# A decoder layer with experts on one core: the tile loop's boundary, the drain's order, and who numbers the tiles

## What is computed

```
xn = _rms_norm(x, scale)
ids = jnp.argmin(_dist2(xn, centroids), axis=-1)
out = jnp.zeros_like(x)
for e in range(N_EXPERTS):
    h = jnp.einsum('bsd,dh->bsh', xn, up_w[e])
    a, g = jnp.split(h, 2, axis=-1)
    y = jnp.einsum('bsh,hd->bsd', a * jax.nn.silu(g), down_w[e])
    out = jnp.where((ids == e)[..., None], y, out)
return out + skip
```

## Time and profile before

| | |
|---|---|
| median of 3 runs | 1331.92 us (1331.41 to 1334.74) |
| the profiled execution, its own time | 1330.11 us |
| its span, first to last instruction | 1328.4 us |
| mean granted TensorE clock | 0.958 |
| busy: TensorE / VectorE / ScalarE / GpSimd | 90% / 64% / 47% / 32% |
| phase 1 without its last two turns | 0 to about 1016 us |
| turns B + 2 and B + 3 | about 1016 to 1062 us |
| routing | about 1062 to 1087 us |
| tiles | about 1087 to 1328 us |

### The profile page before, as it was taken

How to read it: one execution, slowest core, us unless ns; L and a number is a source line. 1 busy time by engine, 2 the same in 40 slices (tenths; PEclk the granted TensorE clock), 3 DMA queues, 4 the chain that set the end, 5 groups by cost and what they waited for, 6 DMA issues and landing times.

```text
span 1328.4 us, 29974 instructions
## 1 busy us (share of the span) xinstructions
PE 1193.5 (90%) x9698; PEld 950.0 (72%) x9699; DVE 847.7 (64%) x2193; ACT 626.5 (47%) x1297; POOL 419.5 (32%) x714
## 2 busy tenths in 40 slices
PE   5496999999999999999999999999997438898887
PEld 4274878777787878778787877778786327777776
DVE  4737667777777867777787777777764752322232
ACT  3426455564746556464746556474634412222222
POOL 2310314232231423233141423223132424444543
PEclk9598999999999999999999999999999559999999
DMA  8502530303123130303213030312257001212221
GB/s 268 130 1 112 222 112 17 113 16 111 47 79 108 34 111 16 111 16 111 79 48 126 16 111 16 111 44 91 89 194 258 31 25 53 65 61 65 62 64 42
DMA packets 51769, 112.30 MB, mean 85 GB/s; under 512 B 7333, under 2 KB 38863, under 8 KB 44944
## 3 DMA queue, kind: packets, MB, share of 16 engines
q1 hardware_dynamic: 45456, 96.81, 21.6%
q0 software_dynamic: 5616, 14.43, 3.7%
q10 hardware_dynamic: 656, 0.52, 0.1%
HBM read 89.72 MB, written 22.94 MB: 85 GB/s over the span
## 4 chain that ended last, share of the span: by engine, by line
PE 76%; DVE 10%; issue 6%; ACT 5%; POOL 2%; DMA 1%; DVEq 0%; ACTq 0%; SPq 0%; POOLq 0%
PE bank L1623 69%; PE bank L1658 3%; DVE a_p L1376 2%; PE bank L1824 2%; ACT shared L867 2%; PE bank L1997 1%; ACT a_p L862 1%; PE bank L1964 1%; POOL shared L979 1%; DVE shared L1549 1%; DVE b_ql L1274 1%; DVE a_split L1301 0%; DVE a_split L1302 0%; DVE a_split L1300 0%; DVE a_ss L1311 0%
## 5 line engine op out<-in xcount | busy, mean ns | idle before, releaser
L1623 PE MATMUL bank<-shared 128*128 128x256 f32 (+4 forms) x1728 | 323.1, 379 | 23.6 <-DVE shared L1549 13.6
L1623 PEld LDWEIGHTS bank<-shared 128*128 128x128 f32 (+2 forms) x1728 | 223.0, 168 | 84.7 <-issue 44.8
L1376 DVE TENSOR_TENSOR a_p<-a_p,eb 128x385 f32<-128x385 f32 x256 | 125.9, 555 | 75.4 <-ACT a_p L862 75.4
L1043 POOL TENSOR_SCALAR a_rz<-a_ms 128x2 f32<-128x2 f32 x16 | 3.1, 192 | 407.0 <-ACT a_sq L890 407.0
L862 ACT ACTIVATE a_p<-bank 128x385 f32<-128x385 f32 x256 | 105.1, 504 | 44.7 <-PE bank L1623 44.6
L1586 DVE TENSOR_TENSOR shared<-bank,shared 128x512 f32<-128x512 f32 x39 | 27.0, 692 | 121.7 <-ACT shared L928 121.7
L867 ACT ACTIVATE shared<-bank 128x512 f32<-128x512 f32 x128 | 66.1, 603 | 36.2 <-PE bank L1623 36.2
L1337 DVE TENSOR_REDUCE shared<-bank 128x2 f32<-128x512 f32 x128 | 79.5, 686 | 1.2 <-PE bank L1623 1.2
L928 ACT ACTIVATE shared<-bank 128x512 f32<-128x512 f32 x39 | 23.3, 597 | 112.7 <-PE bank L1623 112.7
L1023 POOL TENSOR_TENSOR a_split<-a_sq,a_split 128x256 f16<-128x256 f32 x64 | 42.8, 700 | 103.2 <-ACT a_split L809 103.2
L1623 PE MATMUL bank<-up_hi,m_xhi 128*128 x156 | 53.2, 422 | 24.2 <-issue 24.2
(11 more groups left out here) (252 smaller groups left out, 2935.8 us busy)
## 6 DMA issues: line engine op xcount, KB each, us to landing
w_low<-low_w SPq DMA_DIRECT2D x44, 1024.0 KB, 4.8
up<-in_L_ffn_up_w SPq DMA_DIRECT2D x8, 1024.0 KB, 14.4
x_in<-in_x SPq DMA_DIRECT2D x16, 256.0 KB, 2.7
shared<-in_ctx SPq DMA_DIRECT2D x16, 256.0 KB, 3.1
rows_x<-shared SPq DMA_DIRECT2D x16, 256.0 KB, 5.8
rows_skip<-shared SPq DMA_DIRECT2D x16, 256.0 KB, 6.1
down<-in_L_ffn_down_w SPq DMA_DIRECT2D x8, 512.0 KB, 12.5
toep<-a_hT SPq DMA_DIRECT2D x1, 3072.0 KB, 10.2
```

What stands on the lines that cost most here:

```text
L1376: tt(a_p[:, n_ % NPA], a_p[:, n_ % NPA], eb[:, n_], ALU.mult).then_inc(sig["a_p"], 1)
L1623: return mm(out, lhsT=lhsT, rhs=rhs, start=first, stop=last, **kw)
```

## The change

In the drain, DRAIN_PLAN has only the eighths of D.out, so that TensorE runs all eight without a break, and "rows" and "distances" of batch 14 follow behind them. VectorE's nearest() for batch 14 moves behind the last statistics of batch 15, to where three rests stood. Six rests stand ahead of L1346 in turn B + 2, and none behind; turn B + 3 has four, one fills VectorE's wait in the routing, and five (before: one) stand behind the routing. ScalarE's roundings are moved along. In the routing, VectorE makes the first half of number itself, as one instruction, ScalarE the second as one, and in_row is made by four float32 instructions of 128x1024 in place of 32 in float16. In the tile loop, TensorE's turn_hidden of tile 1 and transpose_in of the next step's tile 1 move from the end of a step to the start of the next, behind its choose() calls.

```diff
-DRAIN_PLAN = [("lengths", "C", 0), ("out", "D", 0), ("out", "D", 1), ("out", "D", 2), ("rows", "C", 0), ("out", "D", 3)]
-DRAIN_PLAN += [("out", "D", 4), ("distances", "C", 0), ("expert", "C", 0), ("out", "D", 5)]
+DRAIN_PLAN = [("lengths", "C", 0)] + [("out", "D", n) for n in range(6)]
...
@@ ScalarE, turn B + 2
-                round_up_weights(range(2))
+                round_up_weights(range(3))
...
-                round_up_weights(range(2, 4))
+                round_up_weights(range(3, 4))
                 scaled_rows()
...
                 if what == "rows":
                     evacuate(it, "C.xn", c_xnT[:].rearrange("p c s -> p (c s)"))
-                    if it.first == B + 2:
-                        after(act, "c_nx", c)
-                        round_up_weights(range(4, 5))
...
+            if it.first == B + 2:
+                after(act, "c_nx", c)
+                round_up_weights(range(4, 5))
+                evacuate(it, "C.xn", c_xnT[:].rearrange("p c s -> p (c s)"))
             if Cc:
...
@@ GpSimd, routing
-        pool.wait_ge(s_route, ROUTE_IN_TILE)
-        for half in range(2):
-            part = slice(half * NT // 2, (half + 1) * NT // 2)
-            pool.tensor_tensor(number[:, part, 0], in_tile[:, part],
-                               io_n[:, part].unsqueeze(2).to_broadcast([P, NT // 2, TILES_MAX]),
-                               ALU.mult).then_inc(s_numbered[half], 1)
...
@@ VectorE, turns B + 2 and B + 3
                 if it.first == B + 3:
-                    rest_of_up(range(13, 15))
+                    rest_of_up(range(8, 10))
...
             if it.first == B + 2:
-                rest_of_up(range(0, 3))
+                rest_of_up(range(0, 6))
...
-            if it.first == B + 2:
-                rest_of_up(range(3, 6))
             if it.first == B + 3:
-                rest_of_up(range(12, 13))
+                rest_of_up(range(6, 8))
...
-            if it.first == B + 2:
-                rest_of_up(range(6, 8))
...
-            if it.first == B + 2:
-                rest_of_up(range(8, 9))
...
             if it.first == B + 2:
-                rest_of_up(range(9, 12))
+                nearest()
...
@@ VectorE, routing
         chain(tt(oh[:], bc(expert_of[:], E), over(io_e[:], NT, E), ALU.is_equal))
+        rest_of_up(range(10, 11))
...
+        tt(number[:, :, 0], in_tile[:], bc(io_n[:], TILES_MAX), ALU.mult).then_inc(s_numbered, 1)
         for q in range(QUARTERS):
             part = slice(q * NT // QUARTERS, (q + 1) * NT // QUARTERS)
-            for n in range(part.start, part.stop):
-                ins = ts(in_row[:, n], io_r16[:], r_place[:, 1, n:n + 1], None, ALU.is_equal)
-            chain(ins)
+            chain(tt(in_row[:, part], bc(r_place[:, 1, part], P), over(io_r[:], NT // QUARTERS, P), ALU.is_equal))
...
-        rest_of_up(range(15, 16))
+        rest_of_up(range(11, 16))
...
@@ TensorE, turn B + 2 (turn_rows() and distances() are the old "rows" and "distances")
             if Dd:
                 out_eighth(7)
+            if it.first == B + 2:
+                turn_rows()
+                distances()
...
@@ TensorE, a step of the tiles
-            def turn_hidden(u):
-                after_tile(pe, "m_h", k, u)
-                after_tile(pe, "m_hT", k, u, 0)
+            def turn_hidden(u, back):
+                after_tile(pe, "m_h", k, u, 1 - back)
+                after_tile(pe, "m_hT", k, u, -back)
...
             choose(0, 2 * k)
             if further:
                 choose(-1, 2 * k - 1)
+                turn_hidden(1, 1)
+                if n == 2:
+                    transpose_in(k, 1)
             up_tile(0)
...
-            turn_hidden(0)
+            turn_hidden(0, 0)
             if nxt > 0:
                 transpose_in(k + 1, 0)
             if n == 2:
                 up_tile(1)
             down_tile(0, 0)
-            if n == 2:
-                turn_hidden(1)
-            if nxt > 1:
-                transpose_in(k + 1, 1)
```

More of the change, by code:

```diff
@@ L589, in _build @@
     io_i = sbuf(ctx, "io_i", [P, TILES_MAX])
-    io_r16 = sbuf(ctx, "io_r16", [P, P], F16)
     tri = sbuf(ctx, "tri", [P, P])
     ones_nt = sbuf(ctx, "ones_nt", [P, NT])
-    s_iota, s_numbered = sem("iotas_made"), [sem(f"one_hot_numbered{half}") for half in range(2)]
+    s_iota, s_numbered = sem("iotas_made"), sem("one_hot_numbered")
     BY_TILE = {"m_loaded": 16, "m_skip": 16, "m_row": 1, "m_x": 1, "m_xT": 1, "m_xl": 1, "m_up": 1, "m_silu": 1,
@@ L914, in _ @@
         act.wait_ge(s_route, ROUTE_IN_TILE)
-        for half in range(2):
-            part = slice(half * NT // 2, (half + 1) * NT // 2)
-            nc.scalar.activation(number[:, part, 1], in_tile[:, part], ACT.Copy, scale=io_p[:, 0:1]
-                                 ).then_inc(s_numbered[half], 1)
+        nc.scalar.activation(number[:, :, 1], in_tile[:], ACT.Copy, scale=io_p[:, 0:1]).then_inc(s_numbered, 1)
         def transposed(k, u):
@@ L1076, in _ @@
                            channel_multiplier=-1).then_inc(s_iota, 1)
-        pool.wait_ge(s_iota, 8)
-        pool.tensor_copy(io_r16[:], io_r[:]).then_inc(s_iota, 1)
-        pool.wait_ge(s_route, ROUTE_IN_TILE)
-        for half in range(2):
-            part = slice(half * NT // 2, (half + 1) * NT // 2)
-            pool.tensor_tensor(number[:, part, 0], in_tile[:, part],
-                               io_n[:, part].unsqueeze(2).to_broadcast([P, NT // 2, TILES_MAX]),
-                               ALU.mult).then_inc(s_numbered[half], 1)
         def gather(dst, src, rows, name, u):
@@ L1505, in _ @@
         after(dve, "c_expert", B - 1)
-        dve.wait_ge(s_iota, 9)
+        dve.wait_ge(s_iota, 8)
         link = [0]
@@ L1853, in out_eighth, with turn_rows, distances @@
                     ins.then_inc(f_sem("D.out"), 1)
+            def turn_rows():
+                after(pe, "c_rows", c, T)
+                transposes(it, "C.xn", c_rows)
+            def distances():
+                taken(pe, it, "C.xn")
+                ps = claim(pe, it, "C.dist")
+                for t in range(T):
+                    for c_ in range(C):
+                        ins = product(ps[:, t * E:(t + 1) * E], c_xnT[:, c_, tok(t)], cent_t[:, c_], c_ == 0,
+                                      c_ == C - 1)
+                ins.then_inc(f_sem("C.dist"), 1)
             for what, st, n in plan_of(it):
@@ L1872, in turn @@
                 if what == "rows":
-                    after(pe, "c_rows", c, T)
-                    transposes(it, "C.xn", c_rows)
+                    turn_rows()
                 if what == "distances":
-                    taken(pe, it, "C.xn")
-                    ps = claim(pe, it, "C.dist")
-                    for t in range(T):
-                        for c_ in range(C):
-                            ins = product(ps[:, t * E:(t + 1) * E], c_xnT[:, c_, tok(t)], cent_t[:, c_], c_ == 0,
-                                          c_ == C - 1)
-                    ins.then_inc(f_sem("C.dist"), 1)
+                    distances()
             if A:
@@ L1944, in _ @@
         product(bank[1][:, 0:NT * E], ones[:], flat).then_inc(s_pp, 1)
+        pe.wait_ge(s_numbered, 2)
         for n in range(NT):
-            if n % (NT // 2) == 0:
-                pe.wait_ge(s_numbered[n // (NT // 2)], 2)
             if n % (NT // QUARTERS) == 0:
```

## The result

The changed kernel takes 1295.58 us (median of 4 runs, 1294.54 to 1297.53), the kernel before 1331.66 us beside it (4 runs, 1328.1 to 1334.74). The ratio is 0.9732, 95% interval 0.9705 to 0.9759: 36.1 us faster, 2.7%. The profiled execution took 1294.54 us with a span of 1292.8 us.

What follows compares the result with a forecast made beforehand. TensorE was taken to bound the tiles, losing 24.2 us of issue waits, and chained VectorE and GpSimd steps the drain. Drain 6.0, routing -0.4 and tiles 27 summed to 32.6 us, giving a median of 1299 us, range 1293 to 1313.

Steps and rivals of the forecast that it cites:

- The forecast case: Whole kernel: branch and reads hidden, median 1299 us, between 1293 and 1306; chance 0.58.
- The tile loop: TensorE's step boundaries: 28.5 us at stake in branch and expert reads, less 1.5, so 27 us gained.
- The 1.5 taken off for the wait in a register instruction: Tile loop: 0.1 us lost in each of 15 looped steps, the wait for m_h standing ahead of tile 1's transposes.
- The argument from two rows: TensorE's queue runs ahead: a mid-step read and phase 1's loop branch show no pause, so the new place hides both.
- The bound of 2.39 us: Tile boundary: branch and two reads took at most 2.39 us, six transposes included; one read guessed at about 0.7.
- the queue runs only partly ahead: Rival, tile loop: about half of the 1.66 us per boundary stays, + 13 us, near 1312; chance 0.20.
- slower: Rival, tile loop: branch and reads not hidden at all, 0.7 us more per boundary, 1339 us in all; chance 0.04.
- The drain up to the stores: Turn B + 2: D.out undivided ends earlier, VectorE then waits for the store landing at 1043.4, not 1048.28; 4.8 us gained.
- GpSimd's last chain: Between drain and routing: nearest() beside the chain in place of three rests, 3.71 us for 5.74; 2.0 us gained.
- the extra rest in turn B + 3: One more rest ahead of nearest(), partly hidden by VectorE's wait for the lengths: 0.8 us lost, between 0 and 1.2.
- Routing: Five instructions for 32 small in_row ones, 1.3 us gained; five rests behind the routing, 1.7 us lost.
- the gathers starve: Rival, first tile: GpSimd's gather held until the last of five rests behind the routing, + 3 us, near 1302; chance 0.12.

Runs made afterwards that it cites:

- experiment 1: The kernel before with only TensorE's tile step of the change: 1302.92 us against 1331.42 us, ratio 0.9795.
- experiment 8: The changed kernel with TensorE's steps of the tile loop written out, so without the loop's branch: 1297.91 us.
- experiment 5: The changed kernel with two more unused reads of a tile's expert per step on TensorE: 1297.93 us.
- experiments 4 and 7: Both on the kernel before: 4 with two more unused reads per step, 1370.52 us; 7 with TensorE's tile steps written out, 1316.91 us against 1327.14 us.
- experiment 6: The changed kernel with four more unused reads of a tile's expert per step on TensorE: 1320.74 us.
- experiment 2: The changed kernel with its tile-step part taken back, leaving drain and routing: 1325.55 us against 1331.42 us, ratio 0.996.
- experiment 3: The kernel before with only the routing's new number and in_row instructions: 1331.5 us in one execution; in_tile to sorted_row 10.47 us, before 11.79.
- Experiment 10: The changed kernel with three rests in VectorE's wait for the stores, one fewer in turn B + 3, three behind the routing: 1294.99 us.
- experiment 9: The changed kernel with ScalarE's fifth rounding moved behind C.xn's evacuation and c_x2's scaling: 1300.82 us; b_q add to first transposes 66.21 us, changed kernel 68.18.

## Why the prediction was right

The forecast case came, at 1295.6 us where 1299 was given, inside the forecast's own 1293 to 1306.

- *What bounds the kernel.* TensorE's pauses at the boundaries were the loss in the tiles, and once they were gone TensorE was busy for 178 of 178 us, at a clock of 1.00 as before.
- *The tile loop*, forecast 27, measured 27.6 (both traces) and 28.5 (experiment 1, medians). 28.5 at stake was right within 1 us. The 1.5 taken off for the wait in a register instruction was wrong: the waits came, 0.16 us each, and cost nothing (experiment 8). Without it 28.5 stands against 27.6. From the first turn_hidden to the last, 28.3 us were gained (223.95 before, 195.63 after); behind it 0.75 were lost (8.94 in place of 8.19), which the sum didn't have. The last tile's add on VectorE waited for TensorE before, and now for a gather that GpSimd issued:

```profile
1323.60 0.42 DVE L1596 TENSOR_TENSOR shared<-bank,shared 128x256 f32<-128x256 f32 x1 [2.70 <-PE bank L1623]
```

```profile
1288.04 0.42 DVE L1574 TENSOR_TENSOR shared<-bank,shared 128x256 f32<-128x256 f32 x1 [2.66 <-DMA shared<-rows_skip,shared]
```

- *Why it is hidden.* The argument from two rows (one read in mid-step, phase 1's branch) is borne out by experiment 5. The bound of 2.39 us for branch and two reads was parted by experiments 4 and 7: 0.68 for the loop's end, 0.66 for a further read in the open. My guess of 0.7 for a read was near. The rival *the queue runs only partly ahead* falls, and so does *slower*; experiment 6 says how near they were: 1.4 us of room in a step. (The pauses weren't alike: 1.36 to 1.42 us inside the loop, 0.68 to 1.13 at the other five boundaries. The sum took their total, so this moved nothing.)
- *The drain up to the stores*, forecast 4.8, measured 5.19 in this pair of profiles and 4.1 by the means of experiment 2. The end of the new order came as worked out. But 1048.28, from which the 4.8 were taken, held 28 matmuls at the lower clock for 9.54 us, and in two of five profiles they took 5.38 and 6.38: that both profiles of this pair fit so well is partly luck, and the width that the forecast gave to the drain didn't have this in it. GpSimd's chain beside six rests took 8.32 us from L981 to L1330, before 5.78 beside the three: 2.5 more, as said (2.6). D.out took 7.07 us, forecast 6.9. On the clock of before it ended at 1031.9 + 2.4 = 1034.3, 0.9 later than I had put it, and this moved nothing, since the stores end that part.
- *GpSimd's last chain*, forecast 2.0, measured 2.04; *the extra rest in turn B + 3*, forecast 0.8 lost, measured 0.5.
- *Routing*: in_row and number 1.3 gained (experiment 3 too), and 1.77 lost behind it where 1.7 was forecast. The rival *the gathers starve* falls: TensorE didn't wait for them. But its ground was half right. Three gathers in a row were each held by 0.7 to 1.1 us, and not only one. The Trainium skill, page "SBUF — State Buffer", section "Who interferes with whom", has both the rule that a VectorE instruction with two SBUF inputs contends with GpSimd instructions that read SBUF, and the inference that descriptor writing isn't blocked. The rows agree with the first, by up to one rest of 1.16 us for each gather, and not with a gather that passes untouched. Experiment 10 bears it out: with three rests in place of five the third gather took 0.95 us in place of 1.95.
- *What the sum left out.* 32.6 us were forecast from the changed parts, and these gave 27.6 + 6.35 - 0.7 = 33.2 in this pair of profiles. The first tiles' up products ran longer at the lower clock level (6.89 us in place of 6.18), and 2.4 us more came from turns whose code is the same. With two executions alone I would have credited these to the change. In the profile of before TensorE's clock came back to its upper level later around 115 us (0.57 against 0.72 granted from 110 to 122 us), and turn 2 began 2.2 us later (134.56 against 132.36):

```profile
110.00:122.00 12.00, 8.52 (x120) 4.88 (x121) 8.25 (x14) 7.26 (x19) 0.00 (x0) 0.72 0.43 176
```

```profile
132.36 0.60 PE L1636 MATMUL bank<-ident,a_xl 128*128 128x128 f32 x4
```

(a window and a line of the timeline of the profile after). That the lower clock made the 2.2 us is likely and not shown. Over all profiles, kernels with the same code up to there came to the b_q add between 1010.45 and 1019.02 us. Of the 8.6 us between the changed kernel and experiment 9, 8.3 were there already at the first turn's transposes (85.97 and 94.31). That is variation of the execution, larger than every term of the drain.

## What to carry to other kernels

In this kernel register work and loop ends on TensorE's queue cost nothing where TensorE had matmuls queued and the next instruction waited for another engine anyway; they cost their full length behind the last thing that was waited for. How much room such a place has can be measured by putting unused reads there until a pause appears. For small terms, compare stretches that begin and end at the same instructions in both traces, and not whole times, when the unchanged part varies by more than the term. And take them from several profiles: the old drain's stretch itself differed by 3.6 us between profiles of the same code, the new one's by 0.5.

## What was not expected of the hardware

- Two more reads per step in the open cost 37.9 us and not 25.0: with pauses of 2.1 to 2.7 us the up products behind 8 of 19 boundaries ran at the 1.2 GHz level, 1.3 us or more each, and with pauses of 1.4 us behind none.
- The same 28 matmuls, behind waits of 4.26, 4.36 and 2.99 us, took 9.54, 6.38 and 5.38 us in three profiles, at granted clocks of 0.56, 0.84 and 1.00.
- The end of a hardware loop cost TensorE 0.68 us, as much as a read of a register from SBUF (0.66 us).
- GpSimd's gathers took 1.67 to 2.08 us beside VectorE's two-input rests, and 0.94 to 0.96 right behind the last rest, with one, three or five rests.
- The unchanged turns ahead of the drain differed by up to 8.6 us between executions.
